# A Mamba scan woven into a mixture-of-experts FFN: gate and up projections evacuated by ScalarE from two bank pairs, recurrence steps cut into half units

## The reference, cut to what matters

```python
xn = layernorm(x)                                  # x: (4, 4096, 2048) f32
# branch 1: selective scan, state of 16 per channel
delta = softplus(xp[..., :64] @ W_dt.T + b_dt)     # xp = xn @ W_x.T
for n in range(16):                                # per channel d, over time t
    h[t] = exp(delta[t] * A[n]) * h[t-1] + delta[t] * B[t, n] * xn[t]
    y[t] += h[t] * C[t, n]
y += xn * D
# branch 2: 32 experts, 8 of them weighted per token, all computed densely
for e in range(32):
    out += (silu(xn @ wg[e]) * (xn @ wu[e])) @ wd[e] * w_e[:, None]
x = x + y + out
```

## Time and profile before

| what | value |
| --- | --- |
| median of 3 runs | 15729.37 us (15619.63 to 15747.23) |
| own time of the profiled execution | 15729.37 us |
| its span on the slowest core (core 1) | 15727.8 us |
| spans of all cores | 15011.8 to 15727.8 us |
| busy share: TensorE matmul, VectorE, ScalarE | 66%, 46%, 15% |
| TensorE waits on DMA of down weights | 1469.1 us, 480 times |

### The profile page before, as it was taken

One profiled execution on the slowest core, in us unless ns is written; L12 is line 12 of the kernel. 1 busy time (PEld: TensorE's weight loads), 2 busy tenths in 40 slices (PEclk: granted clock), 3 DMA queues, 4 the chain that ended last, 5 costly groups with the idle time before them and its releaser, 6 DMA issues.

```text
span 15727.8 us, 129189 instructions; the slowest of 8 cores (15011.8 to 15727.8 us)
## 1 busy us (share of the span) xinstructions
PE 10414.1 (66%) x38800; PEld 4306.8 (27%) x38800; DVE 7292.2 (46%) x9945; ACT 2424.5 (15%) x3010; POOL 959.3 (6%) x1798
## 2 busy tenths in 40 slices
PE   2220000288777788887888438888888888888886
PEld 1110000133333333333333223333333333333332
DVE  2238888744444444444444324444444444444443
ACT  1113333311111111111111001111111111111110
POOL 0000000000000000000000000000000000000000
PEclk9999999999899899998877557777777777788776
DMA  1002222244444444444433203333333333343333
GB/s 46 35 28 75 74 74 74 76 80 76 78 82 79 84 79 78 81 79 74 74 72 73 76 26 71 72 73 71 71 72 72 72 72 71 71 78 75 71 72 82
DMA packets 507420, 1117.25 MB, mean 71 GB/s; under 512 B 57296, under 2 KB 188624, under 8 KB 500336
## 3 DMA queue, kind: packets, MB, share of 16 engines
q0 software_dynamic: 258272, 604.75, 23.9%
q1 hardware_dynamic: 248464, 504.23, 10.8%
HBM read 1687.90 MB, written 25.49 MB: 109 GB/s over the span
## 4 chain that ended last, share of the span: by engine, by line
PE 56%; DMA 22%; DVE 12%; issue 6%; ACT 4%; DVEq 0%; ACTq 0%; SPq 0%; POOLq 0%; POOL 0%
PE pb_a L168 19%; PE pb_g L168 17%; PE pb_u L168 17%; DMA wds<-wd 11%; DMA B_sb<-rows_scr 8%; DVE hsc L391 4%; DVE bx L388 1%; PE pb_sm L168 1%; DMA x_tile<-xm 1%; ACT abar L383 1%; PE pb_b L228 1%; ACT L383 1%; ACT xf L230 1%; PE pb_dl L168 1%; DVE xnT L236 1%
## 5 line engine op out<-in xcount | busy, mean ns | idle before, releaser
L168 PE MATMUL pb_a<-harena,wds 128*128 128x512 bf16 x12288 | 3774.3, 481 | 1765.2 <-DMA wds<-wd 1469.1
L168 PE MATMUL pb_g<-xnT,wgs 128*128 128x512 bf16 x12288 | 3193.0, 420 | 253.8 <-DVE g_sb L513 253.8
L168 PE MATMUL pb_u<-xnT,wus 128*128 128x512 bf16 x12288 | 3099.5, 411 | 4.2 <-DMA wus<-wu 4.2
L168 PEld LDWEIGHTS pb_a<-harena,wds 128*128 128x128 bf16 x12288 | 1413.9, 118 | 4126.4 <-issue 3703.6
L391 DVE TENSOR_TENSOR_SCAN hsc<-abar,carry,bx 128x1024 bf16<-128x1024 f32 x1024 | 2406.6, 2350 | 198.4 <-ACT abar L383 105.8
L383 ACT ACTIVATE abar<-delta,A_sb 128x1024 f32<-128x1024 bf16 x1024 | 1176.4, 1149 | 5285.9 <-DVE hsc L391 5190.4
L168 PEld LDWEIGHTS pb_g<-xnT,wgs 128*128 128x128 bf16 x12288 | 1288.9, 106 | 2043.8 <-issue 1436.7
L567 DVE TENSOR_TENSOR acc<-acc,pb_a 128x512 f32<-128x512 f32 x1024 | 703.9, 687 | 2402.3 <-PE pb_a L168 2382.5
L168 PEld LDWEIGHTS pb_u<-xnT,wus 128*128 128x128 bf16 x12288 | 1276.0, 104 | 1698.4 <-issue 1050.7
L517 DVE CAST u_sb<-pb_u 128x512 bf16<-128x512 f32 x768 | 531.1, 691 | 2124.5 <-PE pb_u L168 2111.4
L522 ACT ACTIVATE sg_sb<-g_sb 128x512 bf16<-128x512 bf16 x768 | 483.6, 630 | 4201.0 <-DVE u_sb L517 4199.2
(11 more groups left out here) (66 smaller groups left out, 2966.4 us busy)
## 6 DMA issues: line engine op xcount, KB each, us to landing
B_sb<-rows_scr SPq DMA_DIRECT2D x1024, 256.0 KB, 3.3
wgs<-wg POOLq DMA_DIRECT2D x384, 512.0 KB, 5.3
wus<-wu POOLq DMA_DIRECT2D x384, 512.0 KB, 5.5
wds<-wd POOLq DMA_DIRECT2D x1024, 192.0 KB, 3.8
C_sb<-rows_scr SPq DMA_DIRECT2D x512, 256.0 KB, 3.3
x_tile<-xm SPq DMA_DIRECT2D x32, 1024.0 KB, 5.7
x_tile<-xq SPq DMA_DIRECT2D x16, 1024.0 KB, 4.9
wb<-rows_scr SPq DMA_DIRECT2D x64, 256.0 KB, 4.0
```

Source lines behind the costliest of these rows:

```text
L168: s2=stop: t.matmul(o, l, r, start=s1, stop=s2, skip_group_check=True),
```

## The change

Three things are edited. In `pair`, gate and up results go alternately to the bank pairs `pb_g`/`pb_u` and `pb_b0`/`pb_b1`, and ScalarE instead of VectorE copies them to SBUF, so that the matmul waits refer to `Sm`. `mamba_nstep` gets a parameter `part`: part 0 holds the loads, the Exp, the first multiply, the scan and the carry, part 1 the multiply with C and the sum into `ybuf`; `mamba_units` makes two units of each step, which gives 34 instead of 18. In `out_assembly` the transposes also wait for ScalarE. `drip`, its table and its condition are as before.

```diff
--- before.py
+++ after.py
@@ -362,8 +362,8 @@
                  v.tensor_mul(dxt, delta, xs), [("Sm", sdl)], "Vm")
         ms["dl_war"] = b.c("Vm")
 
-    def mamba_nstep(chunk_tag, dt, n, do_y):
-        if True:
+    def mamba_nstep(chunk_tag, dt, n, do_y, part=None):
+        if part in (None, 0):
             ci = dt * NST + n
             rb = 0 if chunk_tag[0] == "c" else 64 + 16 * int(chunk_tag[1])
             sl_ = n % 2
@@ -379,7 +379,6 @@
                                  rows_d[n_:n_ + 1, :].broadcast_to([P, C])),
                      [("Vm", ms.get(f"Cw{sl_}", 0)),
                       ("RS", ms.get(f"rows_{chunk_tag}", 0))], "BW", 16)
-            brc = b.c("BW")
             b.op("s", lambda s, i=ci, s2=sl_: s.activation(
                 abar[:, s2 * C:(s2 + 1) * C], delta,
                 AF.Exp, scale=A_sb[:, i:i + 1]),
@@ -394,6 +393,9 @@
             ms[f"abar_war{sl_}"] = b.c("Vm")
             b.op("v", lambda v, i=ci: v.tensor_copy(carry[:, i:i + 1],
                                                     hsc[:, C - 1:C]), [], "Vm")
+        if part in (None, 1):
+            sl_ = n % 2
+            brc = b.c("BW")
             if do_y:
                 if n == 0:
                     b.op("v", lambda v, s2=sl_: v.tensor_mul(
@@ -417,7 +419,10 @@
     def mamba_units(chunk_tag, dt, do_y):
         u = [lambda: mamba_prologue(chunk_tag, dt)]
         for n in range(NST):
-            u.append(lambda n=n: mamba_nstep(chunk_tag, dt, n, do_y))
+            u.append(lambda n=n: mamba_nstep(chunk_tag, dt, n, do_y,
+                                             part=0))
+            u.append(lambda n=n: mamba_nstep(chunk_tag, dt, n, do_y,
+                                             part=1))
         if do_y:
             u.append(lambda: mamba_epilogue(dt))
         return u
@@ -488,12 +493,15 @@
                 uslot, usem = load_gu_col("wu", wu_d, wus, e, ic)
                 for sl in range(2):
                     j2 = (ic * 2 + sl) % 2
-                    pg = [pb_g, pb_b0][0]
-                    pu = [pb_u, pb_b1][0]
+                    pg = [pb_g, pb_b0][j2]
+                    pu = [pb_u, pb_b1][j2]
                     for hc in range(16):
                         w_ = [(f"WG{gslot}", gsem), ("Vm", xn_ok)]
                         if hc == 0:
-                            w_.append(("Vm", ms.get("g_evac0", 0)))
+                            w_.append(("Sm", ms.get(f"g_evac0_{j2}", 0)))
+                            if j2 == 1:
+                                w_.append(("Sm", ms.get("bcS0", 0)))
+                                w_.append(("Vm", ms.get("bcV0", 0)))
                         mm(pg[:], wgs[gslot][:, hc * 128:(hc + 1) * 128],
                            xnT[:, hc * C + sl * 512: hc * C + (sl + 1) * 512],
                            hc == 0, hc == 15, w_, "Tm" if hc == 15 else None)
@@ -503,26 +511,28 @@
                     for hc in range(16):
                         w_ = [(f"WU{uslot}", usem)]
                         if hc == 0:
-                            w_.append(("Vm", ms.get("u_evac0", 0)))
+                            w_.append(("Sm", ms.get(f"u_evac0_{j2}", 0)))
+                            if j2 == 1:
+                                w_.append(("Sm", ms.get("bcS1", 0)))
+                                w_.append(("Vm", ms.get("bcV1", 0)))
                         mm(pu[:], wus[uslot][:, hc * 128:(hc + 1) * 128],
                            xnT[:, hc * C + sl * 512: hc * C + (sl + 1) * 512],
                            hc == 0, hc == 15, w_, "Tm" if hc == 15 else None)
                     tu = b.c("Tm")
                     if sl == 1:
                         ms[f"free_wu{uslot}"] = tu
-                    b.op("v", lambda v, j=j2, p_=pg: v.tensor_copy(
+                    b.op("s", lambda s, j=j2, p_=pg: s.copy(
                         g_sb[:, j * 512:(j + 1) * 512], p_[:]),
-                        [("Tm", tg), ("Sm", ms.get(f"silu{j2}", 0))], "Vm")
-                    ms["g_evac0"] = b.c("Vm")
-                    b.op("v", lambda v, j=j2, p_=pu: v.tensor_copy(
+                        [("Tm", tg), ("Sm", ms.get(f"silu{j2}", 0))], "Sm")
+                    ms[f"g_evac0_{j2}"] = b.c("Sm")
+                    b.op("s", lambda s, j=j2, p_=pu: s.copy(
                         u_sb[:, j * 512:(j + 1) * 512], p_[:]),
-                        [("Tm", tu), ("Vm", ms.get(f"h1_{j2}", 0))], "Vm")
-                    ms["u_evac0"] = b.c("Vm")
-                    vgu = b.c("Vm")
+                        [("Tm", tu), ("Vm", ms.get(f"h1_{j2}", 0))], "Sm")
+                    ms[f"u_evac0_{j2}"] = b.c("Sm")
                     b.op("s", lambda s, j=j2: s.activation(
                         sg_sb[:, 0:512],
                         g_sb[:, j * 512:(j + 1) * 512], AF.Silu),
-                        [("Vm", ms.get("sg_war", 0)), ("Vm", vgu)], "Sm")
+                        [("Vm", ms.get("sg_war", 0))], "Sm")
                     ms[f"silu{j2}"] = b.c("Sm")
                     ssl = b.c("Sm")
                     b.op("v", lambda v, j=j2: v.tensor_mul(
@@ -591,7 +601,8 @@
                          i_=acc[:, dc * C + tt * 128: dc * C + tt * 128 + 128]:
                          t.transpose(o, i_, ident),
                          [("Vm", vacc), ("Vm", ms.get(f"bcV{d8 % 2}", 0)),
-                          ("Sm", ms.get(f"bcS{d8 % 2}", 0))], "Tm")
+                          ("Sm", ms.get(f"bcS{d8 % 2}", 0)),
+                          ("Sm", s_dscr)], "Tm")
                     ttp = b.c("Tm")
                     b.op("v", lambda v, s_=sl, d8_=d8, dc_=dc: v.tensor_add(
                         out_tile[:, d8_ * 128:(d8_ + 1) * 128], s_,
```

## The result

| | before | changed |
|---|---|---|
| median of 13 runs each | 15784.56 us | 17300.99 us |
| lowest to highest | 15404.02 to 16080.31 | 16476.05 to 17775.34 |
| the profiled execution: time, span | 15729.37, 15727.8 | 16476.05, 16474.5 |
| VectorE busy | 7292.2 | 6229.7 |
| ScalarE busy | 2424.5 | 2993.7 |

The changed kernel is slower: ratio 1.044, 95% interval 1.036 to 1.052. The ratio compares fast runs alone: those of the changed kernel (16476.05 and 16511.56) have no lower clock by the mean clocks of their cores, those of the kernel before lie near 15800 at that ratio and so have some (a run of it without any took 15127), and the two medians, with it in most runs, stand at 1.096.

What follows compares the result with a forecast made beforehand. TensorE, busy 66% with gaps, was the bound. Pairs +1503, chunk starts -54 and last scans +188 gave +1637 on 15729.37, so 17366 us, taken as 17300; range 16590 to 17650.

Steps and rivals of the forecast that it cites:

- The end at 2.8: End of each gate and up phase: the wait before the first down matmul falls from 9.21 to 2.8 us.
- the transposes' 97: After each chunk's last scan, the first transpose waits for all of VectorE: some 97 us, twice.
- a surcharge of 816 us: Extra time of core 1's 17 slower pairs from the lower clock; a twelfth of it covers the 66 us taken off.
- my first rival: The lower clock disappears, as idle cores release it: all cores end near 16590 us; lower clock mostly gone, chance 0.15.
- I leave it as it is: Down phase, bound by weight loads in 480 waits of 3.1 us: no change from the edit.
- Up by as much: ScalarE's busy time rises by as much as VectorE's falls, some 1060 us.
- The second small wait: Ninth group of a pair: its bank comes free about 0.5 us late, as the second Silu needs VectorE's `harena` product.
- My bound for the unknown copy: ScalarE's 512-column copy, taken as 0.69 us, could be 0.3 to 0.9; this or step error: 25 to 50 us either way.
- The third: Rival: the interleaving works, only finer; 15412 us, faster by 2%; chance 0.02 together with the fourth.
- the fourth: Rival: the scan in one piece stays hidden because copies find their way past; 15399 us; chance 0.02 together with the third.
- The second, spreading to 18000: Rival: a longer run spreads the lower clock to all pairs of core 1, 18000 us; beyond 17600 chance 0.12.
- part of the clock back: While a core idles 65 of some 425 us, others of its die may regain clock; the forecast goes from 17366 to 17300.

Runs made afterwards that it cites:

- e1_condition: The changed kernel with the second half of `drip`'s condition taken out, so its 34 units are placed; 15645.96 us, beside 15956.8 of the kernel before.
- e6_norows: e4_hdone with 14 of 16 loads of B and C rows of each main-chunk scan left out; 15315.5 us, beside 15869.47 of the kernel before.
- e4_hdone: e1_condition, with the first down matmul waiting only for the last `harena` product, not all VectorE work recorded; 15710.1 us.
- e2_units_only: The kernel before with an empty unit behind each scan step, 34 units in all; 17975.5 us, beside 15956.8 of the kernel before.
- z_before: The kernel before with gate, up and down weights all zero; median 15124.66 us.
- e3_banks_only: The changed kernel with one unit per step as before (18 units), so bank pairs and ScalarE copies alone; 15901.7 us.
- z_e1: e1_condition with gate, up and down weights all zero; median 14625.92 us, 0.967 of z_before.
- z_e4: e4_hdone with gate, up and down weights all zero; median 14467.05 us, 0.9565 of z_before.

## Why the prediction came out as it did

**Right: the mechanism and its size.** The condition places nothing, the scan lies in one piece, TensorE waits for a copy on a ScalarE that is itself waiting. The long wait was put at 65 us and is 64.92 in pair 2 (66.4 on average); TensorE was to resume 83.6 us after the last down matmul and does so 83.55 after 3346.54; VectorE was to be through at 97.9 and is at 97.8; steps 5.64 us apart are 5.63 (3422.50 to 3428.13). The end at 2.8 is 2.73, the transposes' 97 is 95.0, VectorE lost 1062 us of busy time (1060 predicted). The waits sum to 2072.9 where I wrote 1950: 30 long ones make 1991 and not 1950, the one behind the prefix pass 48.59, and 26 small ones at the ninth group of a pair 33. e1_condition, which removes the condition alone, shows the cause: 178.3 us per phase where 178.5 was expected.

**The step that failed: the clock.** "I take 17300" rests on the lower clock staying with the changed kernel, at a surcharge of 816 us for 17 pairs of which only a twelfth was taken off. The profiled execution has none of it, at 16476.05 us, and another ended at 16511.56 with the same mean clocks. That is my first rival, "the lower clock disappears", with 16590 and a chance of 0.15, whose other number, 1541 us for core 5, compares with a measured 16337.3 - 15047.1 = 1290. The surcharge is not a property of the kernel that one profile could show: 7 of 26 dies of the changed kernel ran without it and the others with a share that differs, with die spans from 16670 to over 17600 us. The traces show where it stands, and the last section works it out: where all four cores of a die are at matmuls at the same time, which depends on how far apart its two pairs of cores started. My argument against the rival, that core 5's die "ran four such cores without it", took for granted that the four ran at the same time; that is not shown, and the traces speak against it.

The median of all 13 runs (17300.99) meets the forecast by luck, because two errors cancel: the time without the lower clock was put at 16590 and is about 16494, and what the lower clock adds was put at 17300 - 16590 = 710 and is 807 in the median. What I should have given is two times, one for each condition, and a ratio for each: 1.09 without the lower clock on either side (die spans of about 16405 against 15060), 1.096 between the medians.

**A smaller term that failed: the down phase.** "I leave it as it is" was wrong by about 8.6 us a pair. The whole sum for core 5, which never had the lower clock on either side, goes term by term like this:

| term, core 5 | predicted | measured |
|---|---|---|
| start of the first down phase | -38 | -40 |
| 30 gate and up phases | 30 x 47.2 = +1416 | 30 x (241.65 - 193.15) = +1455 |
| 32 down phases | 0 | 32 x (149.67 - 158.28) = -275 |
| from chunk 0's last down matmul to chunk 1's first | +94 - 25 = +69 | 875.9 - 813.5 = +62 |
| behind the last down matmul | +94 | 235.4 - 147.1 = +88 |
| sum | +1541 | +1290 |

All of the difference but some 25 us is the down phase. The changed kernel moves the row loads away from the down weights as well as the scan. e6_norows shows that the loads have a price, 4.4 of the 7.0 us that part e4_hdone and the changed kernel over all cores; the scan's own 0.9 is within what the cores differ by, and the rest stays open. On core 5 the wait ahead of each group of 24 fell from 3.14 to 2.88 us, 14 x 0.26 = 3.6 of the 8.6 us; the groups themselves are shorter by 14 x 0.13 = 1.8 (6.79 to 6.66), the first 30 matmuls by 1.9 (8.96 to 7.07) and the first wait for weights by 0.8 (4.29 to 3.45). I had counted the loads of a moved step only where they arrive, not where they no longer disturb.

**ScalarE.** "Up by as much" (1060 us) was wrong: it is 569. A copy takes 0.585 us, not 0.69, so 1536 of them make 899 us. Against it stand 256 fewer table loads of 1.283 us, 328 us, since Exps and Silus no longer alternate: of 321 on core 1, 65 are left on core 6, 32 of them ahead of the prologues and 32 ahead of the first Silus. Copies off the waited-for path cost nothing in the span.

**Small terms.** The second small wait was put at 0.5 us; on core 6 it is 0 to 2.0 us, 1.3 on average in the 26 pairs that have it. The phase came to 241.65 where 240.7 was predicted. The loads of `wb` were in time, as expected. My bound for the unknown copy (25 to 50 us either way) was wide enough.

**The rivals.** The third (finer interleaving works) and the fourth (the scan is hidden) are refuted by the timeline and by e1_condition, which is what the third had assumed and which runs that way, 3.5% below the kernel before at full clock (14537 against some 15060). The second, spreading to 18000, is not excluded in single executions (the highest run is 17775.34), but no run reached 18000. The forecast's reason, that idle time would give "part of the clock back", can be looked for in e2_units_only, whose cores stand idle for up to 89.5 us per pair: core 0 is at 0.81 from 9500 to 9630 and at 1.00 from 9785 to 9793, so the clock does come back inside the part that the cores share, but for a few us at a time. For the changed kernel itself no trace shows it.

## What to carry to other kernels

Count what a guard condition admits before judging what an edit does to an interleaving: splitting units made a comparison of a table length with a unit count go negative, and two good changes (second bank pair, copies on an idle engine) were buried under it. An engine's low busy share says nothing about its queue: the copy stood behind 16 Exps on an engine that was 18% busy and mostly waiting for another. Two bank pairs buy two groups' time, not the time of a row of steps. Where the clock differs between executions, compare dies at the same clock, or zero the operands, before a few per cent are believed; and look at all cores of a die before one core's clock is called the kernel's.

## What the hardware showed that I had not expected

**The lower clock depends on the data.** With zero weights no die of 16 executions shows it, with real weights most do. The Trainium skill ("TensorE: Matmul & The Clock Gate", the part on the HAM clock gate, in its note on the peak-current limiter) says that all-zero operands don't trip it; the four zero-weight kernels agree, 15108 to 15133 us for z_before.

**It stands where both pairs of a die's cores are at matmuls.** Within die 0 of the kernel before, cores 0 and 1 have the lower clock in the same stretches of their own time, cores 2 and 3 in the same ones as each other, but the two pairs in different ones. Set 4645 us apart, they fall on one another:

| core 1, us | its clock | core 2, us | its clock | core 2 + 4645 |
|---|---|---|---|---|
| 2978 to 7623 | 0.90 | | | |
| 7623 to 8762 | 0.76 | 2978 to 4116 | 0.75 | 7623 to 8761 |
| | | 4116 to 4754 | 0.91 | 8761 to 9399 |
| 9399 to 13950 | 0.76 | 4754 to 9157 | 0.76 | 9399 to 13802 |
| 13950 to 14423 | 0.89 | | | |
| 14423 to 15561 | 0.76 | 9777 to 10915 | 0.76 | 14422 to 15560 |
| | | 10915 to 15484 | 0.91 | 15560 to 20129 |

(These means contain waits at 0.50; between waits the clock of core 1 is 0.81 from 14440 to 14600.) At 8762 core 1 ends the matmuls of its first chunk, at 9399 it begins those of the second, near 15561 it ends them; core 2 does the same near 9157, at 9777 and near 15484, and begins its first pair at 2978. Every other edge of one core is such an event of the other, to within 1 us, but for 13950, which is some 100 us late. So the lower clock fits the time in which both pairs of cores are at gate, up and down matmuls, if cores 2 and 3 started 4645 us after cores 0 and 1. No trace has a common time for the cores, so the shift is inferred; but all twelve dies that have the lower clock in a trace of these kernels show the same picture to within 150 us, with shifts from 3540 to 11889 us. In e4_hdone it is 10989: cores 0 and 1 have the lower clock from 2985 to 3351, their first matmuls, and cores 2 and 3 from 13974 to 14340, their last. With real weights, a die without it would then be one whose pairs started so far apart that their matmuls never met. The same note of the Trainium skill says that three cores of a die with dense matmuls are enough. The stretches agree: with one pair at matmuls the clock is full, with both it is the lower one (three cores alone no run here shows). Why the pairs start apart is open.

**It eats gains.** At the lower clock e1_condition's gate and up phase is 214 us, 35.7 above its 178.3, while that of the kernel before is some 28 above its 193. The kernel with fewer gaps pays more for the lower clock in each such phase. The medians agree, though they also carry the shares that each kernel's few runs happened to have: those of e1_condition, e3_banks_only and e4_hdone stand at 0.981, 0.997 and 0.985 of the kernel before, but z_e1 and z_e4 at 0.967 and 0.9565 of z_before.

**Row loads of 256 KB slow the weight loads on another queue.** With them each wait ahead of a group of 24 is 3.18 us (e4_hdone), with 14 of 16 left out 3.02 (e6_norows), although the queues are different ones (SP's and POOL's) and the DMA engines are less than half busy (DMA share 0.40 in the earlier trace rows).

**The copy is quicker on ScalarE.** A 128x512 copy from PSUM to bf16 took 585 ns there and 691 ns on VectorE before the change (0.69 us in the earlier trace rows).
